# Attention and recurrence in one TensorE order: dense products over all heads of a trip, a block's steps over four trips

## The chip, the cores and the metric

One core of a Trainium2 chip runs the kernel. The metric is the time of one execution on the device, in microseconds (us). TensorE (PE) multiplies, VectorE (DVE) and ScalarE (ACT) do elementwise work, GpSimd (POOL) and SyncE (SP) mostly issue DMAs. Each engine takes its own list of instructions in order and waits on semaphores.

## The reference, cut to what matters

```python
# x is [8, 512, 512]; 16 heads of 32; cond is [8, 512]
qkv = x @ c_attn_w + c_attn_b                      # split into q, k_word, v_word
k = concat([cond @ uk_w.T + uk_b, k_word]);  v = concat([cond @ uv_w.T + uv_b, v_word])
scores = einsum('bhqd,bhkd->bhqk', q, k) / sqrt(32)    # causal, the image key is always seen
out = softmax(scores + mask) @ v
x = x + (out @ c_proj_w + c_proj_b)
xw = x @ Wx + b                                     # then 512 steps in sequence, h0 = cond:
h[t] = tanh(h[t-1] @ Wh + xw[:, t])
return x + h
```

Everything is float32; the products with c_attn_w and c_proj_w are made of three products of split operands (high x high, high x low, low x high).

## The kernel before

The 512 positions are four blocks of 128. A *trip* is one block of one pair of batches: 16 trips, trip g has block g // 4 and pair g % 4. A trip has 32 *heads* (two batches x 16 heads), so there are 512 heads in all, u = 32 g + h.

Work of a trip: `xsplit` splits x into high and low parts (ACT, then VectorE); `q` and `k` are projected in four chunks c of four heads each, `imgscore` scores chunk c against the image key; `v` are four products (two batches e, two halves). q and k go through DRAM (`kq_dram`) and come back as tiles of four heads of one batch: `kqload` of group 8 g + 4 e + c, two tile buffers. Values are stored by GpSimd (`vstore`) and come back by `vload`, three buffers, eight groups a trip. Per head: `score` (L839), shift against mask and image score (VectorE, L687), exp (ACT, L551), `turn` (transposes of the probabilities, L847, four heads later), a copy (L696 or L558), and per four heads `pv` (L860, ten heads later). Per batch: `total` (VectorE, L705 to L713, needs the trip before's x1 stores, as L713 overwrites their buffer), `imgturn`, `rowturn`, `norm`. When a trip's heads are done, `finish` does it inside the next trip: `proj` (four products), `x1n` (two transposes, copied by ACT, stored by GpSimd at L500), `wx` (four products into xw) or, in the last block, `keep` (a GpSimd copy, L490).

The recurrence has 512 `step`s. A step is 16 small products on TensorE (L924), a transpose (L751) and an add (L761) on VectorE, a tanh on ACT (L593); the next needs its result. Steps of block b need the x1 and xw of its four trips, so blocks 0 to 2's steps (128 each) run beside the attention of the next block; block 3's run alone at the end (the tail), with their own wx products (L916). After each 16 steps `out` turns and stores the states. wx of trip 4(b+1)+r overwrites the xw cells that steps 32 r to 32 r + 31 of block b read.

The order is planned by hand. `main_order` (L61) lists the events of all heads with a weight each (estimated us on TensorE). There, before the change, `project(g)` (L65) is the whole projection of a trip, `side` the list of dense events still to be placed: project(g + 1) is set at h = 0 and held until h = 10, when finish(g - 1) is put ahead of it; from there to h = 31 the list is spread over the heads. So heads 0 to 9 of a trip carry no dense event, heads 10 to 31 carry up to two each. `flush` (L82) adds the loads that are ready. `order` (L140) places each group of 32 steps, evenly by weight, between `finished` of trip group + 3 and the first wx of trip group + 4 (L149 to L158), and then gives every engine its own list, sorted by the planned clock plus a lag per engine and kind (`LAGS`, L45). SyncE's list has the loads and the q/k stores (L427, L439, L449), GpSimd's the mask loads (L476 to L482, two per trip, one for each batch of the next trip, after heads 15 and 31), vstore (L497), x1 stores (L500), keep and the output (L467, L505). Both wait in order, so what stands behind a waiting entry waits too.

Of the kernel before, what the change touches and what calls it, by code (L numbers as in the profile page):

```python
# [5 lines left out]
P = 128  # L6
# [44 lines left out]
    "SP": {"xload": 0.8, "vimgload": 0.5, "q": 1.3, "k": 1.3, "kqload": 0.0, "vload": 0.5},  # L51
# [5 lines left out]
def block_of(g):  # L57
    return g // PAIRS


def main_order():  # L61

    out = []

    def project(g):  # L65
        return ([("xsplit", g, k, 0.0) for k in range(2)]
                + [e for c in (0, 1) for e in (("q", g, c, 1.4), ("k", g, c, 1.4), ("imgscore", g, c, 0.5))]
                + [("v", g, i, 1.4) for i in range(4)] + [("vstore", g, 0, 0.0)]
                + [e for c in (2, 3) for e in (("q", g, c, 1.4), ("k", g, c, 1.4), ("imgscore", g, c, 0.5))])

    def finish(g):
        last = "keep" if block_of(g) == BLOCKS - 1 else "wx"
        return ([("proj", g, c, 1.4) for c in range(C)] + [("xload", g + 2, 0, 0.0)] * (g + 2 < TRIPS)
                + [("x1n", g, e, 0.85) for e in range(2)]
                + [(last, g, c, 1.7 * (last == "wx")) for c in range(C)] + [("finished", g, 0, 0.0)])

    out += [("xload", 0, 0, 0.0), ("xload", 1, 0, 0.0), ("mskload", 0, 0, 0.0), ("mskload", 0, 1, 0.0),
            ("vimgload", 0, 0, 0.0), ("vimgload", 0, 1, 0.0)] + project(0)
    side, loads = [], [("kqload", group, 0, 0.0) for group in range(TILES)]
    loads += [("vload", group, 0, 0.0) for group in range(VTILES)]  # L80

    def flush():  # L82

        ready = {(kind, g, i) for kind, g, i, _ in out[-200:]}
        for load in list(loads):
            trip, c = load[1] // 8, load[1] % C
            after = ("k", trip, c) if load[0] == "kqload" else ("vstore", trip, 0)
            if after in ready or load[1] % 8 > C:
                out.append(load)
                loads.remove(load)  # L90

    for u in range(HEADS + 2 * H):
        g, h = divmod(u, UNITS)
        if h == 0 and g < TRIPS:
            out += side
            flush()
            side = project(g + 1) if g + 1 < TRIPS else []
        if h == 10 and g:
            side = finish(g - 1) + side
# [886 lines left out]
```

## Time and profile before

| | us |
|---|---|
| median of 3 runs | 1851.33 (1847.14 to 1851.88) |
| the profiled execution | 1850.24, span 1848.5 |
| TensorE busy | 1657.4 (90%) |
| VectorE / ScalarE / GpSimd busy | 889.7 / 708.1 / 149.4 |
| mean granted TensorE clock | 0.948 |

"Busy" is the time with at least one instruction of the engine running; matmuls overlap, so 90% is not 90% of the peak. The clock is a share of 2.4 GHz: 1.00 is the full level, 0.50 the lower one of 1.2 GHz. The first attention head starts at 76 us, the last trip's heads end at 1527 us, and the tail of 128 steps starts at 1568 us.

### The profile page before, as it was taken

The page shows a single profiled execution, that of the slowest core. Times are in us where ns is not written, and L with a number is a line of the kernel's source. Part 1 is how long each engine was busy: PE and PEld are TensorE (multiplying, and loading weights), DVE is VectorE, ACT ScalarE, POOL GpSimd, SP SyncE. Part 2 cuts the span into 40 slices and gives each one's busy share as a digit, 9 for nine tenths or more (in the row PEclk, how much of TensorE's full clock was granted, in tenths as well). Part 3 has the DMA queues.
Part 4 walks back from the last instruction along what each step waited for, and adds up shares of the span by engine and source line. Part 5 has one row for each costly group of instructions (what it writes and reads, how often), then busy time and mean ns, then how long its engine had stood idle before and what let it go on. Part 6 is the DMA issues. An engine that isn't in the chain of part 4 may idle for free.

```text
span 1848.5 us, 67862 instructions
## 1 busy us (share of the span) xinstructions
PE 1657.4 (90%) x29292; PEld 1389.1 (75%) x29292; DVE 889.7 (48%) x2986; ACT 708.1 (38%) x2205; POOL 149.4 (8%) x248
## 2 busy tenths in 40 slices
PE   3788888989898998989899998989999887999997
PEld 2777777878787887878787886878778666888875
DVE  4254345454555454655645555556656563222222
ACT  2254444444443444444444444444444442111110
POOL 1001000000000000001011000001000000000000
PEclk7879888999999999999999998999999999999998
DMA  6455346444445355565555456566656640100000
GB/s 233 143 149 157 114 139 170 127 131 120 122 118 135 103 134 129 139 141 137 150 138 148 116 136 151 140 161 157 159 145 161 137 111 25 27 15 17 26 15 20
DMA packets 228442, 221.67 MB, mean 120 GB/s; under 512 B 22952, under 2 KB 187048, under 8 KB 227632
## 3 DMA queue, kind: packets, MB, share of 16 engines
q1 hardware_dynamic: 211568, 175.86, 36.7%
q0 software_dynamic: 16576, 41.46, 8.0%
q8 instruction: 233, 3.82, 0.9%
q14 instruction: 65, 0.53, 0.1%
HBM read 141.45 MB, written 75.76 MB: 118 GB/s over the span
## 4 chain that ended last, share of the span: by engine, by line
PE 72%; DMA 9%; DVE 8%; issue 5%; ACT 4%; SPq 3%; POOL 0%; DVEq 0%; POOLq 0%; ACTq 0%
PE rec L924 22%; PE turned L847 8%; PE dense L380 7%; DMA kq<-kq_dram 6%; PE dense L381 6%; PE dense L382 6%; PE dense L895 5%; PE scores L839 4%; PE pv L860 4%; PE scores L924 3%; DVE pre L751 3%; PE pv L878 2%; ACT hist L593 2%; DVE probs L687 1%; SPq L427 1%
## 5 line engine op out<-in xcount | busy, mean ns | idle before, releaser
L924 PE MATMUL rec<-wh,hist 128*8 128x128 f32 x14336 | 487.9, 277 | 29.7 <-ACT hist L593 23.3
L924 PEld LDWEIGHTS rec<-wh,hist 128*8 128x8 f32 x14336 | 356.2, 94 | 112.6 <-ACT hist L593 66.1
L551 ACT ACTIVATE probs<-probs,nmax 128x128 f32<-128x128 f32 (+3 forms) x512 | 287.2, 561 | 187.2 <-DVE nmax L687 179.6
L593 ACT ACTIVATE hist<-pre 128x32 f32<-128x32 f32 x512 | 131.7, 257 | 573.4 <-DVE pre L761 331.9
L687 DVE CUSTOM_DVE_ANT_0 probs<-scores,msk,nimg 128x128 f32<-128x128 f32 (+3 forms) x512 | 276.2, 545 | 131.2 <-PE scores L839 128.6
L839 PE MATMUL scores<-kq 96*128 96x128 f32 (+3 forms) x512 | 212.5, 420 | 82.6 <-DMA kq<-kq_dram 81.0
L751 DVE STREAM_TRANSPOSE pre<-rec 128x128 f32<-128x128 f32 x448 | 141.4, 316 | 295.6 <-PE rec L924 292.2
L847 PE MATMUL turned<-ident,probs 128*128 128x128 f32 x1280 | 250.0, 296 | 1.4 <-DVE probsT L696 1.0
L847 PEld LDWEIGHTS turned<-ident,probs 128*128 128x128 f32 x1280 | 150.3, 145 | 69.2 <-issue 56.7
L839 PEld LDWEIGHTS scores<-kq 96*128 96x128 f32 x512 | 107.7, 211 | 109.5 <-DMA kq<-kq_dram 86.8
L696 DVE COPY probsT<-turned 128x128 f32<-128x128 f32 (+3 forms) x256 | 124.8, 487 | 112.2 <-PE turned L847 111.6
L380 PE MATMUL dense<-xT_hi,wqkv_hi 128*128 128x256 f32 x512 | 152.0, 297 | 28.8 <-DVE xT_lo L653 23.9
L558 ACT COPY probsT<-turned 128x128 f32<-128x128 f32 (+3 forms) x256 | 107.6, 420 | 128.9 <-PE turned L847 128.0
L381 PE MATMUL dense<-xT_lo,wqkv_hi 128*128 128x256 f32 x512 | 146.0, 285 | 0.0
L382 PE MATMUL dense<-xT_hi,wqkv_lo 128*128 128x256 f32 x512 | 145.5, 284 | 0.0
L380 PEld LDWEIGHTS dense<-xT_hi,wqkv_hi 128*128 128x128 f32 x512 | 98.5, 192 | 38.2 <-issue 30.6
L860 PE MATMUL pv<-probsT,vbuf 128*32 128x128 f32 x2560 | 102.4, 290 | 0.3
L381 PEld LDWEIGHTS dense<-xT_lo,wqkv_hi 128*128 128x128 f32 x512 | 98.6, 193 | 0.6
L382 PEld LDWEIGHTS dense<-xT_hi,wqkv_lo 128*128 128x128 f32 x512 | 98.4, 192 | 0.0
L551 ACT ACTIVATION_READ_ACCUMULATOR probs<-probs,nmax 128x1 f32 x512 | 96.0, 188 | 0.0
L895 PE MATMUL dense<-x1T,wx 128*128 128x256 f32 x384 | 90.3, 383 | 0.7 <-ACT x1nat L586 0.3
L761 DVE TENSOR_TENSOR pre<-pre,xw 128x32 f32<-128x32 f32 x384 | 83.1, 216 | 13.1
(119 smaller groups left out, 2291.1 us busy)
## 6 DMA issues: line engine op xcount, KB each, us to landing
kq<-kq_dram SPq DMA_DIRECT2D x96, 320.0 KB, 5.7
kq<-kq_dram SPq DMA_DIRECT2D x96, 256.0 KB, 4.8
kq<-kq_dram SPq DMA_DIRECT2D x96, 192.0 KB, 3.7
kq_dram<-qs_hi SPq DMA_DIRECT2D x128, 128.0 KB, 2.1
kq_dram<-ks_hi SPq DMA_DIRECT2D x128, 128.0 KB, 3.2
kq<-kq_dram SPq DMA_DIRECT2D x96, 128.0 KB, 2.6
xin<-x SPq DMA_DIRECT2D x32, 256.0 KB, 3.1
kq_dram<-qs_lo SPq DMA_DIRECT2D x64, 128.0 KB, 2.4
```

Source lines behind the costliest of these rows:

```text
L380: pe.matmul(out, hi, moving_hi, start=first, stop=False)
L381: pe.matmul(out, hi, moving_lo, start=False, stop=False)
L382: return pe.matmul(out, lo, moving_hi, start=False, stop=last)
L551: act.activation(probs[:, g % PROBS, 0:n], probs[:, g % PROBS, 0:n], ACT.Exp, scale=-1.0, bias=nmax[:, e, h:h + 1], accum_out=rowsum[:, e, ...
L593: act.activation(hist[:, g // HALF % 2, :, :, g % HALF], pre[:, :, 0:B], ACT.Tanh).then_inc(h_ready, 1)
L687: dve.tensor_tensor_reduce(out=probs[:, g % PROBS, 0:n], in0=scores[g % 2][:, 0:n], in1=msk[:, e, 0:n], scale=-SCALE, scalar=nimg[:, trip ...
L751: dve.transpose(pre_all, rec_bank(g)[:, 0:P]).then_inc(rec_turned, 1)
L839: pe.matmul(scores[g % 2][:, 0:n], heads_tile(group)[0:3 * Q, j, 0:P], heads_tile(group)[0:3 * Q, j, P:P + n], start=True, stop=True).then ...
L847: last = pe.transpose(turned[g % 2][:, P * k:P * k + P], probs[:, g % PROBS, P * k:P * k + P], ident[:])
L860: last = pe.matmul(pv[Q * j:Q * j + Q, P * c:P * c + P], vtile[g % VTILES][:, k, Q * j:Q * j + Q], probsT[:, (HC * g + j) % TURNED, P * k: ...
L895: last = pe.matmul(d[:, 0:2 * P], wx[:, f, P * i:P * i + P], x1T[:, f, :], start=f == 0, stop=f == C - 1)
L924: last = pe.matmul(d[Q * j:Q * j + B, 0:P], hist[:, before // HALF, f, :, before % HALF], wh[:, f, P * j:P * j + P], start=f == 0 and not ...
```

## The change

Dense events are placed in two parts. Heads 0 to 9 of trip g now take values(g, 0), chunk(g, 3), values(g, 1): the trip's own four value products and its last chunk of q and k. Heads 10 to 31 take finish(g - 1), the split of the next x (ahead of the last two wx) and chunks 0 to 2 of trip g + 1, one event per head. Before the first head only chunks 0 to 2 of trip 0 are projected. Each value half is stored by itself, with a semaphore of its own. Loads are listed as soon as what they read is listed. A block's 128 steps are spaced evenly by weight over one window, from `finished` of trip 4 b + 3 to the first wx (or keep) of trip 4 b + 7; where a group's cells are about to be overwritten, its remaining steps are placed just before. Weights and three of SyncE's lags are changed, and the shift waits for its own chunk's image scores.

```diff
--- before.py
+++ after.py
@@ -48,7 +48,7 @@
     "ACT": {"xsplit": 0.0, "q": 0.2, "k": 0.2, "score": 0.8, "turn": 0.2, "imgprob": 0.2, "imgturn": 0.2,
             "rowturn": 0.2, "norm": 0.6, "wx": 0.2, "x1n": 0.2, "step": 0.7},
     "POOL": {"mskload": 0.0, "keep": 0.2, "vstore": 1.0, "x1n": 0.8, "finished": 0.0, "out": 1.0},
-    "SP": {"xload": 0.8, "vimgload": 0.5, "q": 1.3, "k": 1.3, "kqload": 0.0, "vload": 0.5},
+    "SP": {"xload": 0.8, "vimgload": 0.9, "q": 1.3, "k": 1.3, "kqload": 1.4, "vload": 0.5},
 }
 
 DENSE_KINDS = ("q", "k", "v", "imgscore", "imgturn", "rowturn", "proj", "wx", "x1n", "out")
@@ -60,80 +60,79 @@
 
 def main_order():
 
-    out = []
-
-    def project(g):
-        return ([("xsplit", g, k, 0.0) for k in range(2)]
-                + [e for c in (0, 1) for e in (("q", g, c, 1.4), ("k", g, c, 1.4), ("imgscore", g, c, 0.5))]
-                + [("v", g, i, 1.4) for i in range(4)] + [("vstore", g, 0, 0.0)]
-                + [e for c in (2, 3) for e in (("q", g, c, 1.4), ("k", g, c, 1.4), ("imgscore", g, c, 0.5))])
+    out, seen, loads = [], set(), [("kqload", group, 0, 0.0) for group in range(TILES)]
+    loads += [("vload", group, 0, 0.0) for group in range(VTILES)]
+
+    def emit(events):
+
+        for event in events:
+            out.append(event)
+            seen.add(event[:3])
+            for load in list(loads):
+                trip, k = divmod(load[1], 8)
+                if (("k", trip, k % C) if load[0] == "kqload" else ("vstore", trip, k // C)) in seen:
+                    out.append(load)
+                    loads.remove(load)
+
+    def chunk(g, c):
+        return [("q", g, c, 1.5), ("k", g, c, 1.5), ("imgscore", g, c, 0.5)]
+
+    def values(g, e):
+        return [("v", g, 2 * e, 1.5), ("v", g, 2 * e + 1, 1.5), ("vstore", g, e, 0.0)]
+
+    def begin(g):
+        return [("xsplit", g, k, 0.0) for k in range(2)]
 
     def finish(g):
         last = "keep" if block_of(g) == BLOCKS - 1 else "wx"
-        return ([("proj", g, c, 1.4) for c in range(C)] + [("xload", g + 2, 0, 0.0)] * (g + 2 < TRIPS)
-                + [("x1n", g, e, 0.85) for e in range(2)]
-                + [(last, g, c, 1.7 * (last == "wx")) for c in range(C)] + [("finished", g, 0, 0.0)])
-
-    out += [("xload", 0, 0, 0.0), ("xload", 1, 0, 0.0), ("mskload", 0, 0, 0.0), ("mskload", 0, 1, 0.0),
-            ("vimgload", 0, 0, 0.0), ("vimgload", 0, 1, 0.0)] + project(0)
-    side, loads = [], [("kqload", group, 0, 0.0) for group in range(TILES)]
-    loads += [("vload", group, 0, 0.0) for group in range(VTILES)]
-
-    def flush():
-
-        ready = {(kind, g, i) for kind, g, i, _ in out[-200:]}
-        for load in list(loads):
-            trip, c = load[1] // 8, load[1] % C
-            after = ("k", trip, c) if load[0] == "kqload" else ("vstore", trip, 0)
-            if after in ready or load[1] % 8 > C:
-                out.append(load)
-                loads.remove(load)
-
+        return ([("proj", g, c, 1.5) for c in range(C)] + [("xload", g + 2, 0, 0.0)] * (g + 2 < TRIPS)
+                + [("x1n", g, e, 0.55) for e in range(2)]
+                + [(last, g, c, 1.8 * (last == "wx")) for c in range(C)] + [("finished", g, 0, 0.0)])
+
+    emit([("xload", 0, 0, 0.0), ("xload", 1, 0, 0.0), ("mskload", 0, 0, 0.0), ("mskload", 0, 1, 0.0),
+          ("vimgload", 0, 0, 0.0), ("vimgload", 0, 1, 0.0)] + begin(0) + chunk(0, 0) + chunk(0, 1) + chunk(0, 2))
+    side, until = [], 0
     for u in range(HEADS + 2 * H):
         g, h = divmod(u, UNITS)
+        block, h2 = divmod(u, H)
         if h == 0 and g < TRIPS:
-            out += side
-            flush()
-            side = project(g + 1) if g + 1 < TRIPS else []
-        if h == 10 and g:
-            side = finish(g - 1) + side
-        block, h2 = divmod(u, H)
+
+            side, until = values(g, 0) + chunk(g, 3) + values(g, 1), 9
+        if h == 10:
+            side, until = [], UNITS - 1
+            if 0 < g <= TRIPS:
+                side += finish(g - 1)
+            if g + 1 < TRIPS:
+
+                at = max(len(side) - 3, 0)
+                side[at:at] = begin(g + 1)
+                side += chunk(g + 1, 0) + chunk(g + 1, 1) + chunk(g + 1, 2)
         if h2 == 8 and 0 < block <= 2 * TRIPS:
-            out.append(("norm", block - 1, 0, 0.9))
+            emit([("norm", block - 1, 0, 0.9)])
             if block + 1 < 2 * TRIPS:
-                out.append(("vimgload", (block + 1) // 2, (block + 1) % 2, 0.0))
+                emit([("vimgload", (block + 1) // 2, (block + 1) % 2, 0.0)])
         if h2 == 9 and 0 < block <= 2 * TRIPS:
-            out.append(("attnlow", block - 1, 0, 0.0))
-        p = block_of(min(g, TRIPS - 1))
+            emit([("attnlow", block - 1, 0, 0.0)])
         if u >= PV_LAG and (u - PV_LAG) % HC == 0 and u - PV_LAG < HEADS:
-            v = u - PV_LAG
-            out.append(("pv", v // HC, 0, 0.05 + 0.213 * (block_of(v // UNITS) + 1)))
-            if v // HC + VTILES < GROUPS:
-                loads.append(("vload", v // HC + VTILES, 0, 0.0))
+            v = (u - PV_LAG) // HC
+            if v + VTILES < GROUPS:
+                loads.append(("vload", v + VTILES, 0, 0.0))
+            emit([("pv", v, 0, 0.1 + 0.213 * (block_of(v // 8) + 1))])
         if TURN_LAG <= u < HEADS + TURN_LAG:
             v = u - TURN_LAG
-            out.append(("turn", v, 0, 0.11 * (block_of(v // UNITS) + 1)))
+            emit([("turn", v, 0, 0.05 + 0.11 * (block_of(v // UNITS) + 1))])
         if u < HEADS:
-            out.append(("score", u, 0, max(0.11, 0.053 * (p + 1)) + 0.06))
             if u % HC == HC - 1 and u // HC + TILES < GROUPS:
                 loads.append(("kqload", u // HC + TILES, 0, 0.0))
+            emit([("score", u, 0, max(0.11, 0.053 * (block_of(g) + 1)) + 0.1)])
             if h2 == 15 and block + 2 < 2 * TRIPS:
-                out.append(("mskload", (block + 2) // 2, block % 2, 0.0))
+                emit([("mskload", (block + 2) // 2, block % 2, 0.0)])
         if 0 < block <= 2 * TRIPS:
-            out += {1: [("imgprob", block - 1, 0, 0.0)], 2: [("total", block - 1, 0, 0.0)],
-                    4: [("imgturn", block - 1, 0, 0.15)], 5: [("rowturn", block - 1, 0, 0.45)]}.get(h2, [])
-        if g < TRIPS:
-            room = UNITS - 1 - h
-            take = len(side) if room == 0 else -(-len(side) // (room + 1))
-            if h < 10 and g:
-
-                take = 0
-            out += side[:take]
-            side = side[take:]
-        else:
-            out += side
-            side = []
-        flush()
+            emit({1: [("imgprob", block - 1, 0, 0.0)], 2: [("total", block - 1, 0, 0.0)],
+                  4: [("imgturn", block - 1, 0, 0.15)], 5: [("rowturn", block - 1, 0, 0.5)]}.get(h2, []))
+        take = len(side) if g >= TRIPS or h >= until else -(-len(side) // (until + 1 - h))
+        emit(side[:take])
+        side = side[take:]
     return out
 
 
@@ -146,16 +145,18 @@
         if kind in ("wx", "keep"):
             begins.setdefault(g, n)
     place = {}
-    for group in range((BLOCKS - 1) * PAIRS):
-        first, last = ends[group + PAIRS - 1] + 1, begins[group + PAIRS]
+    for b in range(BLOCKS - 1):
+
+        first, last = ends[(b + 1) * PAIRS - 1] + 1, begins[(b + 2) * PAIRS - 1]
         whole = sum(w for *_, w in main[first:last])
         done, n = 0.0, 0
         for at in range(first, last):
             done += main[at][3]
-            while n < STEPS and done >= whole * (n + 0.5) / STEPS:
-                place.setdefault(at, []).append(group * STEPS + n)
+            while n < P and (done >= whole * (n + 0.5) / P
+                             or at + 1 == begins.get((b + 1) * PAIRS + n // STEPS)):
+                place.setdefault(at, []).append(b * P + n)
                 n += 1
-        assert n == STEPS
+        assert n == P
 
     plan = {name: [] for name in ("PE", "DVE", "ACT", "POOL", "SP")}
     clock = 0.0
@@ -169,7 +170,7 @@
                 plan[name].append((clock + lags[kind], kind, g, i))
 
     def step(t):
-        put("step", t, 0, 0.85)
+        put("step", t, 0, 1.05)
         if t % HALF == 1 and t > HALF:
             put("out", t // HALF - 1, 0, 0.5)
 
...
                     trip, k = divmod(g, 8)
                     p, r = divmod(trip, PAIRS)
                     e, c = divmod(k, C)
-                    sp.wait_ge(v_stored, 32 * (trip + 1))
+                    sp.wait_ge(v_stored[e], 16 * (trip + 1))
                     if g >= VTILES:
                         sp.wait_ge(pv_done, g - VTILES + 1)
...
                 elif kind == "vstore":
-                    for n in range(4):
-                        wait_copied(pool, "v", g, n)
-                    for e in range(2):
-                        pool.dma_start(v_dram[2 * r + e, P * p:P * p + P, :], vnew[:, e, :]).then_inc(v_stored, 16)
+                    for n in range(2):
+                        wait_copied(pool, "v", g, 2 * i + n)
+                    pool.dma_start(v_dram[2 * r + i, P * p:P * p + P, :], vnew[:, i, :]).then_inc(v_stored[i], 16)
...
                 elif kind == "v":
                     wait_dense(dve, kind, g, i)
-                    if i == 0:
+                    e, half = divmod(i, 2)
+                    if half == 0:
                         dve.wait_ge(bv_loaded, 16)
                         if g:
-                            dve.wait_ge(v_stored, 32 * g)
-                    e, half = divmod(i, 2)
+                            dve.wait_ge(v_stored[e], 16 * g)
                     cols = slice(half * D // 2, (half + 1) * D // 2)
                     dve.tensor_tensor(vnew[:, e, cols], bank(kind, g, i)[:, 0:D // 2], bv[:, cols], ALU.add
                                       ).then_inc(copied(kind, g, i), 1)
...
                     if h == 0:
                         dve.wait_ge(mask_ready, 2 * trip + e + 1)
-                        wait_copied(dve, "imgscore", trip, C - 2)
-                        wait_copied(dve, "imgscore", trip, C - 1)
+                    if h % HC == 0:
+                        wait_copied(dve, "imgscore", trip, h // HC)
                     dve.tensor_tensor_reduce(out=probs[:, g % PROBS, 0:n], in0=scores[g % 2][:, 0:n],
                                              in1=msk[:, e, 0:n], scale=-SCALE, scalar=nimg[:, trip % 2, e, h:h + 1],
```

## Rows read from the trace of the kernel before

**Rows 1.** The page: busy us by engine, and TensorE's clock in 40 slices.
```profile
PE 1657.4 (90%) x29292; PEld 1389.1 (75%) x29292; DVE 889.7 (48%) x2986; ACT 708.1 (38%) x2205; POOL 149.4 (8%) x248
...
PEclk7879888999999999999999998999999999999998
```

**Rows 2.** TensorE's waits: us in total, times, longest.
```profile
PE scores L839 <- DMA kq<-kq_dram: 81.0, 20, 6.3
PE dense L380 <- DVE xT_lo L653: 23.9, 11, 15.5
PE rec L924 <- ACT hist L593: 23.3, 45, 1.4
```

**Rows 3.** Busy us per stretch, trips 9, 15: PE PEld DVE ACT POOL, clock, DMA, GB/s.
```profile
795.50:900.60 105.10, 99.14 (x1629) 82.68 (x1627) 57.78 (x185) 46.72 (x138) 9.21 (x14) 0.97 0.54 136
...
1436.60:1527.40 90.80, 77.36 (x1429) 60.08 (x1427) 55.20 (x157) 43.69 (x121) 7.11 (x12) 0.94 0.54 124
```

**Rows 4.** TensorE in time (start us, us, line) [idle before], trip 8, heads 0 to 4.
```profile
691.27 0.42 PE L839 MATMUL scores<-kq 96*128 96x384 f32 x1
...
694.06 0.42 PE L839 MATMUL scores<-kq 96*128 96x384 f32 x1
...
695.10 1.06 PE L924 MATMUL rec<-wh,hist 128*8 128x128 f32 x32
701.99 0.69 PE L839 MATMUL scores<-kq 96*128 96x384 f32 x1 [5.82 <-DMA kq<-kq_dram]
```

**Rows 5.** The same stretch: GpSimd's mask load and SyncE's tile loads.
```profile
691.78 0.58 POOL L476 DMA_DIRECT2D msk<-mask  x1
...
692.16 4.08 SPq L439 DMA_DIRECT2D kq<-kq_dram  x6
```

**Rows 6.** Busy us per stretch: the gap of trip 8, and behind it.
```profile
696.20:702.00 5.80, 0.01 (x1) 0.02 (x1) 1.11 (x5) 0.71 (x2) 1.62 (x2) 0.72 1.04 221
702.00:705.60 3.60, 3.60 (x30) 2.92 (x34) 1.25 (x4) 2.36 (x7) 0.00 (x0) 0.50 0.78 154
```

**Rows 7.** TensorE in time, trip 2: a product at the lower and full clock.
```profile
195.95 0.41 PE L382 MATMUL dense<-attnT_hi,wproj_lo 128*128 128x256 f32 x1
196.16 0.41 PE L380 MATMUL dense<-attnT_hi,wproj_hi 128*128 128x256 f32 x1
...
201.26 0.28 PE L381 MATMUL dense<-attnT_lo,wproj_hi 128*128 128x256 f32 x1
201.38 0.28 PE L382 MATMUL dense<-attnT_hi,wproj_lo 128*128 128x256 f32 x1
```

**Rows 8.** Busy us per stretch: one of block 0's four at the lower clock.
```profile
310.00:324.00 14.00, 10.18 (x62) 8.32 (x63) 6.10 (x22) 6.03 (x21) 1.30 (x2) 0.52 0.72 178
```

**Rows 9.** TensorE in time, the drain: two steps with nothing between them.
```profile
1544.18 1.07 PE L924 MATMUL rec<-wh,hist 128*8 128x128 f32 x32
1546.22 1.07 PE L924 MATMUL rec<-wh,hist 128*8 128x128 f32 x32 [0.97 <-ACT hist L593]
```

**Rows 10.** Busy us per stretch: the end of the drain.
```profile
1546.00:1568.00 22.00, 15.40 (x332) 12.30 (x332) 6.65 (x22) 3.37 (x12) 2.56 (x6) 1.00 0.07 26
```

**Rows 11.** Trip 13 in time: head 15's score, GpSimd's mask load, VectorE's L713.
```profile
1269.91 0.47 PE L839 MATMUL scores<-kq 96*128 96x512 f32 x1
...
1271.84 0.54 POOL L476 DMA_DIRECT2D msk<-mask  x1 [1.59 <-DVE nmax L687]
...
1281.39 0.46 POOL L482 TENSOR_TENSOR msk<-msk,causal 128x128 f32<-128x128 f32 x1
...
1282.99 0.43 DVE L713 COPY x1nat<-rinv 128x512 f32<-128x512 f32 x1
```

**Rows 12.** Trip 15 in time, VectorE's wait for the x1 store.
```profile
1490.00 0.43 DVE L713 COPY x1nat<-rinv 128x512 f32<-128x512 f32 x1 [1.72 <-DMA x_dram<-x1nat]
```

**Rows 13.** The page's DMA issues: count, KB each, median us to landing.
```profile
kq<-kq_dram SPq DMA_DIRECT2D x96, 320.0 KB, 5.7
...
x_dram<-x1nat POOLq DMA_DIRECT2D x32, 256.0 KB, 2.6
```

More of the change, by code:

```diff
@@ L315, in attention_recurrence @@
         tile_loaded = [sem(f"tile_loaded{i}") for i in range(TILES)]
-        v_stored = sem("v_stored")
+        v_stored = [sem(f"v_stored{e}") for e in range(2)]
         v_loaded = [sem(f"v_loaded{i}") for i in range(VTILES)]
@@ L508, in _ @@
             pool.wait_ge(out_stored, 16 * OUTS)
-            pool.wait_ge(v_stored, 32 * TRIPS)
+            for e in range(2):
+                pool.wait_ge(v_stored[e], 16 * TRIPS)
             pool.wait_ge(x1_stored, 32 * TRIPS)
@@ L743, in _ @@
                         dve.wait_ge(x1_kept, C * PAIRS)
-                        dve.wait_ge(v_stored, 32 * TRIPS)
+                        for e in range(2):
+                            dve.wait_ge(v_stored[e], 16 * TRIPS)
                     elif g % P == 0:
```

## Prediction, made blind

> **What bounds the kernel now.** I read the busy shares first, then what TensorE waited for, then one trip of the attention in order of time. TensorE is busy 90% of the span and its clock row shows dips all along [rows 1]; no other engine is above 48%. Inside the trips the share is higher still: trip 9 takes 105.10 us with 99.14 busy, at a mean clock of 0.97 [rows 3]. So nearly all that can be won without removing matmuls is TensorE's idle time, and the change removes none: the same products, transposes and steps are issued. The list of its waits says where the idle time is: 81.0 us in 20 waits for a load of the q/k tile, 23.9 us for the low part of x (15.5 of it once, in the set-up), 23.3 us in 45 waits of a recurrence step for the state before it [rows 2].
>
> The tile wait has one place, shown by trip 8 [rows 4]: the first four heads run from 691.27 to 694.06, a step follows at 695.10, and then TensorE is idle 5.82 us, till 701.99. Every later trip has the same gap once. The cause is the order of work: heads 0 to 9 of a trip carry no dense product, so its first four heads pass in some 4 us, while the next tile's load, issued at 692.16 [rows 5] just behind the last chunk's stores and beside a mask broadcast, lands only at 701.99. The DMA engines are full in the gap (share 1.04), and the clock then stays at its lower level for the 3.60 us behind it [rows 6].
>
> **What the order becomes.** Counted from the code: heads 0 to 9 of each trip carry its own four value products and chunk 3 (six products of 1.5 and one image score); from head 10 follow proj, x1n, wx and the next trip's chunks 0 to 2, one event per head. Steps are spaced evenly over four trips.
>
> **1. Tile wait: -73.** Heads 0 to 3 now hold two value products, attention work and three to four steps. A product is 12 matmuls at 0.12 us, 1.43 us, and a step is 1.0 us of TensorE [rows 7, 9], so the four heads take some 5.5 us in block 0 and 9 to 14 later, against some 4 now. A tile load lands in 5.7 us at its largest (320 KB) when it meets no jam [rows 13], and the second tile's load of that trip start, which shared the engines with it, is now issued those many us later. What stays: SyncE's queue now has the value loads, which wait for values stored in this very trip, ahead of the load of group 2; in block 0, where heads are short, I work it out as about 2 us late in each of trips 0 to 3. 81.0 - 8 = 73. Bounds: 2 us left in all (-79), 40 left (-41).
>
> **2. Clock: -13.** At the lower level a dense product's matmuls start 0.21 us apart, at the full one 0.12 [rows 7], so a product costs 1.1 us more. Block 0 has four long stretches at the lower level (the last one in [rows 8]); some nine products lie in the parts behind the waits: 10 us. The short stretch of each later trip [rows 6] holds transposes and steps, which cost nearly the same at either level: 12 x 0.25 = 3. Bounds -5 and -25.
>
> **3. Waits for the low part of x: -7.** The split of x moves ahead of the last two wx products, so two heads and 3.6 us lie before the first q. 23.9 - 15.5 = 8.4 [rows 2], of which I keep 1. Bounds -4, -8.
>
> **4. Waits of steps outside bursts: -11.** By the planner's weights, steps in block 1 now come every 1.71 instead of 1.39, and the last 32 steps of block 2 are not squeezed into trip 15 and the drain (13.4 us of idle time in trip 15, [rows 3]). Of 23.3 us I take half. Bounds 0 and -20.
>
> **5. Bursts of steps: +21.** This speaks against the change. An even spacing over the window of four trips is slower than the old one over each trip, but the 32 steps of a group must be done before wx of the matching trip overwrites their cells, and the placement forces the remainder there. Adding the weights (block 1: 57.0 a trip, window 218.8, 1.709 per step; 45.2 before the first wx) gives 26 steps placed and 6 forced, back to back, in head 16 of trip 5; 4 in trip 6, 3 in trip 7; the same 6, 4, 3 in trips 9 to 11; none in the last block, whose keep copies weigh nothing. Back to back, a step starts 2.04 us after the one before (1544.18 to 1546.22) and needs 1.0 of it [rows 9]: transpose, add and tanh lie between. TensorE issues in order, so everything behind waits: (5+3+2) x 2 = 20 extra x 1.04 = 21. Bounds 15 (something slips between) and 30 (VectorE busy with a shift when the step ends).
>
> **6. GpSimd's queue in mid-trip: +12.** x1n moves from heads 12 and 13 to 14 and 15. The mask load of head 15 has lag 0, x1n's store lag 0.8, so on GpSimd the load now stands ahead of the store, and its issue, wait and two operations hold the queue. In trip 13 head 15's score starts at 1269.91 and GpSimd is through with the mask at 1281.85 [rows 11]; a store behind that lands 2.6 us later [rows 13], at +14.6 us. VectorE's copy L713 at head 18 waits for exactly this store, with scores, transposed copies and steps queued behind it. It stands at 1282.99, +13.1 [rows 11]; without the two products and the output transpose that lie there now, at about +9.5. So VectorE is 5 us late. The trace has one such wait, 1.72 us in trip 15 [rows 12]. By the same working: trips 1 to 3 some 1.1 us, trips 4, 8 and 12 about 2, trips 13 and 14 about 5; behind a burst none. Sum 19.7; TensorE's work in hand covers about 1 us of each of the eight: 12. Bounds 0 and 30.
>
> Sum: -73 -13 -7 -11 +21 +12 = -71. The profiled execution took 1850.24 us (span 1848.5); 1850.2 - 71 = 1779.2. The median is 1.1 above it: **1780 us**. SyncE's other moves (kqload's lag 1.4, the image values') come off at nothing: its queue waits on engines now and will again. VectorE's wait for chunk 3's image scores (made in head 5, used in head 12), the two semaphores of stored values (same order on GpSimd) and the one-event-per-head spreading of products, for which two PSUM banks suffice today, are costed at nothing as well: VectorE is busy 55% and ACT 44% of trip 9 [rows 3]; if that cover were gone, each product would cost TensorE up to 1 us of waiting for its bank. The setup gains nothing beyond the first tile wait: six products leave the part before the first head and come back inside trip 0.
>
> A rule that speaks against the bursts: the Trainium skill, "TensorE: Matmul & The Clock Gate", section "A second HAM failure mode: psum-queue depth-cycling", says that frequent micro-idles between groups of matmuls can make the clock swing between its levels. By it a burst would be followed by dense work at 1.2 GHz. The trace does not bear it out: in the drain, with steps waiting on each other and 15.40 of 22 us busy, the clock is 1.00 [rows 10].
>
> **Rivals.**
> A. GpSimd's queue costs nothing and the clock comes back whole: 1780 - 12 - 8 = 1760. For it: TensorE's lead may cover short waits. Against: the 5 us of trips 13 and 14 are too long for that. 0.2.
> B. Half of the tile wait stays, because the value loads block SyncE at trip starts and the jam of mask, stores and loads is as it was. Tile term -41 and clock -5: 1780 + 32 + 8 = 1820. For it: full DMA engines in the gap [rows 6]. Against: twice the time until the tile is due. 0.17.
> C. Each burst drops the clock. Six stretches of the length of rows 6 (6.8 us from the gap's middle), full of dense work at 0.21 instead of 0.12, lose 3 us each: 1780 + 18 = 1798. Against: [rows 10]. 0.08.
> D. Slower: the tile wait moves from group 1 to group 2 of each trip at its full size. Group 2's load stands on SyncE behind value loads that wait for the store of this trip's values; that store stands on GpSimd behind the mask load of head 31. It decides once stored values land later than score 8 less 7 us (load and issue); worse than before from 4.6 us a trip on. Then terms 1 and 2 are zero: 1850 - 7 - 11 + 21 + 12 = 1865, 1866 by the median. Against: between head 31 and score 8 lie 20 us of TensorE work in block 1 and 30 in block 3, mask plus store take 10 to 14. 0.05.
>
> **How the numbers follow.** Forecast 0.5, A 0.2, B 0.17, C 0.08, D 0.05. The range leaves D out and part of A's and B's outer bounds: 1750 to 1824. A measurement can tell 0.3%, 5.5 us, from no change. Faster 0.93 (all but D, less a little for B's tail), same 0.02, slower 0.05.
>
> **What would show it.** Right: TensorE's wait for q/k tiles under 20 us; windows of trips 1 to 15 without the gap after head 3; clock 1.00 through trips 4 to 11; six places with 6, 4, 3 steps 2.04 us apart, in head 16; VectorE's L713 waiting for the x1 store, about 5 us in trips 13 and 14. Wrong: tile waits at another group, long waits of SyncE for stored values with TensorE idle behind them, or a mean clock no higher than before.

## The result: 1800.4 us, and the profile after

The changed kernel takes 1800.41 us (median of 4 runs, 1796.14 to 1802.70) against 1849.24 for the kernel before in the same comparison: a ratio of 0.973, 95% interval 0.971 to 0.976. The forecast was 1780 in a range of 1750 to 1824. The sign and the largest term were right, and the gain was 49 us where 71 were expected. The profiled execution has a span of 1798.5, so against [rows 1]'s span of 1848.5 there are 50.0 us to explain.

The page after: busy us by engine, and TensorE's clock in 40 slices.

```profile
span 1798.5 us, 67877 instructions
...
PE 1634.6 (91%) x29292; PEld 1378.1 (77%) x29292; DVE 888.8 (49%) x2986; ACT 709.9 (39%) x2205; POOL 149.6 (8%) x248
...
PEclk8988989999999999999999999998998999999999
```

Against [rows 1] the matmuls are the same 29292, yet they keep TensorE busy 22.8 us less (1657.4 to 1634.6). That is the clock: by its records TensorE was busy 132 us at the lower level before and is 92 now, and with a step's 1.07 us at the full level for 1.90 at the lower one (rows below) that is some 18 of the 22.8, an estimate. The other 27.2 us are idle time (191.1 to 163.9). The clock row has few dips left, and some of them are new: an 8 in slices 28 and 31, where the row before has nines.

TensorE's waits after, to be read against [rows 2] (us in total, times, longest).

```profile
PE rec L926 <- ACT hist L594: 56.6, 70, 7.8
...
PE scores L841 <- DVE nmax L688: 23.7, 6, 5.6
...
PE scores L841 <- DMA kq<-kq_dram: 13.8, 11, 4.4
...
PE dense L381 <- DVE xT_lo L654: 4.6, 1, 4.6
```

The tile wait fell from 81.0 to 13.8, and the wait for the low part of x from 23.9 to 4.6. What came up is the first two rows: steps waiting for a state (23.3 before, with 1.4 as the longest; 56.6 now, with 7.8) and scores waiting for a shift on VectorE (1.5 in the same view of before, 23.7 now). The changes of these four rows sum to -67.2 - 19.3 + 33.3 + 22.2 = -31.0, near the 27.2 of idle time.

The start of trip 8 after, which answers [rows 4]: TensorE in order of time (start us, us).

```profile
650.89 0.42 PE L841 MATMUL scores<-kq 96*128 96x384 f32 x1
...
652.67 1.07 PE L926 MATMUL rec<-wh,hist 128*8 128x128 f32 x32
...
653.86 0.42 PE L841 MATMUL scores<-kq 96*128 96x384 f32 x1
...
658.67 0.44 PE L841 MATMUL scores<-kq 96*128 96x384 f32 x1
...
659.09 0.42 PE L841 MATMUL scores<-kq 96*128 96x384 f32 x1
...
662.60 0.42 PE L841 MATMUL scores<-kq 96*128 96x384 f32 x1
```

Head 4 now starts 11.7 us after head 0 (9 to 14 were worked out) and waits for nothing. It had been 10.7 us before, 5.8 of them idle. The products that fill this time no longer stand in the rest of the trip.

What took their place is seen in trip 13. GpSimd and VectorE in order of time, and last the step that TensorE resumes with; in brackets the idle time before each and who ended it.

```profile
1235.05 0.54 POOL L477 DMA_DIRECT2D msk<-mask  x1 [1.55 <-DVE nmax L688]
...
1241.66 0.25 DVE L708 RECIPROCAL rinv<-total 128x16 f32<-128x16 f32 x1
...
1242.57 0.45 POOL L483 TENSOR_TENSOR msk<-msk,causal 128x128 f32<-128x128 f32 x1
...
1242.96 0.60 POOL L500 DMA_DIRECT2D x_dram<-x1nat  x1
...
1248.66 0.43 DVE L714 COPY x1nat<-rinv 128x512 f32<-128x512 f32 x1 [6.74 <-DMA x_dram<-x1nat]
...
1250.50 1.90 PE L926 MATMUL rec<-wh,hist 128*8 128x128 f32 x32 [6.10 <-ACT hist L594]
```

And the same stretch by windows (busy us of PE, PEld, DVE, ACT, POOL; then clock, DMA share, GB/s).

```profile
1241.00:1249.00 8.00, 2.31 (x27) 1.43 (x15) 1.23 (x5) 1.35 (x4) 3.47 (x5) 0.74 0.85 222
1249.00:1255.00 6.00, 4.50 (x60) 3.15 (x64) 4.92 (x14) 3.34 (x10) 2.16 (x4) 0.50 0.16 45
1255.00:1262.30 7.30, 7.30 (x141) 6.16 (x134) 4.00 (x12) 3.54 (x11) 0.00 (x0) 0.99 0.57 141
```

GpSimd issues the mask load at 1235.05, waits for it, does its two operations, and only then issues the second of the trip's two x1 stores, at 1242.96. VectorE's copy L714 overwrites what the store reads, so it starts 5.7 us later, at 1248.66, and the shifts, transposes and adds queued behind it hold TensorE for 6.10 us. Behind the gap the clock is at its lower level (0.50) for 6 us. VectorE's row for this wait, over the whole kernel, is this one:

```profile
  DMA x_dram<-x1nat: 44.9, 8
```

There are eight such waits, in trips 1 to 4, 8 and 12 to 14, and before there was only the one of 1.72 us [rows 12].

### The profile page after: what moved, and what is told of

It is laid out like the page before. It is cut to its first block, busy times and chain, and to the rows that moved or that the text cites. A ratio compares the mean times of both kernels' runs of the same rounds, so it can differ in the third digit from the quotient of the medians.

```text
span 1798.5 us, 67877 instructions
## 1 busy us (share of the span) xinstructions
PE 1634.6 (91%) x29292; PEld 1378.1 (77%) x29292; DVE 888.8 (49%) x2986; ACT 709.9 (39%) x2205; POOL 149.6 (8%) x248
## 4 chain that ended last, share of the span: by engine, by line
PE 72%; DVE 9%; DMA 7%; issue 5%; ACT 4%; SPq 2%; POOL 1%; DVEq 0%; POOLq 0%; ACTq 0%
PE rec L926 24%; PE turned L849 8%; PE dense L381 7%; PE dense L382 6%; PE dense L383 6%; PE pv L862 4%; PE scores L841 4%; PE scores L926 3%; PE dense L897 3%; DVE pre L753 3%; ACT hist L594 3%; DMA msk<-mask 2%; DMA x_dram<-x1nat 2%; PE pv L880 2%; DVE probs L688 1%
## 5 line engine op out<-in xcount | busy, mean ns | idle before, releaser
L926 PE MATMUL rec<-wh,hist 128*8 128x128 f32 x14336 | 483.7, 275 | 62.9 <-ACT hist L594 56.6
L849 PE MATMUL turned<-ident,probs 128*128 128x128 f32 x1280 | 241.0, 288 | 1.9 <-DVE probsT L697 0.9
L841 PE MATMUL scores<-kq 96*128 96x128 f32 (+3 forms) x512 | 203.8, 403 | 37.7 <-DVE nmax L688 23.7
L849 PEld LDWEIGHTS turned<-ident,probs 128*128 128x128 f32 x1280 | 145.3, 141 | 65.3 <-issue 55.2
L841 PEld LDWEIGHTS scores<-kq 96*128 96x128 f32 x512 | 102.4, 201 | 58.2 <-DVE nmax L688 27.8
L897 PE MATMUL dense<-x1T,wx 128*128 128x256 f32 x384 | 104.3, 419 | 6.4 <-ACT xw L582 6.4
L862 PE MATMUL pv<-probsT,vbuf 128*32 128x128 f32 x2560 | 98.6, 282 | 1.4 <-DVE x1T L728 1.3
L897 PEld LDWEIGHTS dense<-x1T,wx 128*128 128x128 f32 x384 | 76.9, 209 | 21.7 <-ACT xw L582 9.3
```

The source lines that it names most:

```text
L841: pe.matmul(scores[g % 2][:, 0:n], heads_tile(group)[0:3 * Q, j, 0:P], heads_tile(group)[0:3 * Q, j, P:P + n], start=True, stop=True).then ...
L849: last = pe.transpose(turned[g % 2][:, P * k:P * k + P], probs[:, g % PROBS, P * k:P * k + P], ident[:])
L862: last = pe.matmul(pv[Q * j:Q * j + Q, P * c:P * c + P], vtile[g % VTILES][:, k, Q * j:Q * j + Q], probsT[:, (HC * g + j) % TURNED, P * k: ...
L897: last = pe.matmul(d[:, 0:2 * P], wx[:, f, P * i:P * i + P], x1T[:, f, :], start=f == 0, stop=f == C - 1)
L926: last = pe.matmul(d[Q * j:Q * j + B, 0:P], hist[:, before // HALF, f, :, before % HALF], wh[:, f, P * j:P * j + P], start=f == 0 and not ...
```

## Experiments

Edits are against the changed kernel, except where "before" is said. Ratios are to the kernel before, with 95% intervals.

### The x1 store ahead of the mask load (changed kernel)

```diff
-    "POOL": {"mskload": 0.0, "keep": 0.2, ...
+    "POOL": {"mskload": 2.5, "keep": 0.2, ...
```

> The changed kernel with GpSimd's mask loads 2.5 later in its list, so that both x1 stores stand ahead of the mask load of head 15. Theory: VectorE's wait for the x1 store (44.9 us, 8 times) goes to under 3, and most of it is TensorE time: 23.7 us of waits for VectorE's shifts and some 10 of the step waits, so 1800 - 30 = 1770. Rival (the size in the prediction, 12 us): TensorE's work in hand hides most of it: 1788. A second rival: the masks, now later, are late for the heads: no gain.

Measured: 1744.80, ratio 0.944 [0.941, 0.947], span 1743.1, that is 55 us below the changed kernel, nearly twice what was expected. Its page has this row of busy times:

```profile
PE 1615.2 (93%) x29292; PEld 1366.6 (78%) x29292; DVE 890.1 (51%) x2986; ACT 709.3 (41%) x2205; POOL 151.7 (9%) x248
```

And these are TensorE's first two waits:

```profile
PE rec L926 <- ACT hist L594: 45.0, 72, 1.2
PE scores L841 <- DMA kq<-kq_dram: 13.3, 10, 4.5
```

The longest wait of a step is 1.2 (1.4 before), the scores' wait for a shift is gone from the list, and VectorE's wait at L714 is 0.6 us once. The gain lies where it should: heads 16 to 23 of the eight trips take 21.1, 20.6, 20.2, 24.6, 28.2, 30.7, 26.9 and 29.0 us in the changed kernel, and 14.5, 16.9, 13.9, 17.7, 20.9, 23.6, 18.7 and 19.9 here, a sum of 55 us. Idle time falls by 36.0 (163.9 to 127.9) and busy time by 19.4. In the eight stretches alone idle time falls by 35 and busy time by 20. So a third of the store wait's price was the clock behind each gap.

### No bursts (changed kernel)

Each group's 32 steps are spread up to their own deadline, so none is forced.

```diff
-        first, last = ends[(b + 1) * PAIRS - 1] + 1, begins[(b + 2) * PAIRS - 1]
-        whole = sum(w for *_, w in main[first:last])
...
+        at, n = ends[(b + 1) * PAIRS - 1] + 1, 0
+        for r in range(PAIRS):
+            last = begins[(b + 1) * PAIRS + r]
+            whole, done = sum(w for *_, w in main[at:last]), 0.0
```

> The changed kernel with each group of 32 steps spaced evenly up to its own deadline (the first wx that overwrites its cells), so none is forced: in block 1 the first group gets one step per 1.41 of weight, the others one per 1.78. Theory: the 20 extra steps of the bursts cost 1.04 us each, so the step waits fall from 56.6 to about 35 and the time by 21: 1779. Rival: what the bursts lose is won back in the step-free stretch behind them: no change, 1800.

Measured: 1794.66, ratio 0.970 [0.965, 0.973]: 6 us below the changed kernel where 21 were expected. TensorE's first two waits tell why.

```profile
PE scores L842 <- DVE nmax L689: 40.5, 10, 8.7
PE rec L927 <- ACT hist L595: 30.4, 53, 2.8
```

The steps' waits halved, but the scores' wait for VectorE rose from 23.7 to 40.5. Most of that rise is a change of name: in trips 13 and 14 a step waited 6.1 and 7.8 us for the late store, and now a score waits 8.4 and 8.7 for it. VectorE's own row shows how much more of the late store came up:

```profile
DVE x1nat L715 <- DMA x_dram<-x1nat: 49.2, 10, 7.9
```

Against 44.9 in 8 waits, that is two more, of 1.2 and 2.8 us, in trips 10 and 11: the burst of head 16 had stood ahead of L714 there and had covered the same store. From the first score of trip 4 to that of trip 12 the run is 8.8 us shorter. But it also changed something else: the last block's steps are bound to their trips again, 6 more of them are left behind the last score, and the tail takes 12.3 us more (316.5 against 304.2). So this run doesn't price the bursts, and the next ones have the store first.

### Both together

The two edits above in one kernel.

> Both edits, stores ahead of the mask load and no bursts. Theory: the two costs are apart in place (bursts in trips 5 to 7 and 9 to 11; store waits in the other trips), so the gains add: 1800 - 30 - 21 = 1749. Rival: bursts covered the store wait in their trips, so without them it comes up there, and with the stores first that does not matter; then the second edit alone (e4) gains less than 21 and both together still about 50.

Measured: 1731.99, ratio 0.937 [0.934, 0.941], span 1727.2, 17 us below the expectation. Against the run with the store first alone it is 13 us by the medians. So the bursts cost more than the 6 of the run above showed, though here too the tail is 12.5 us longer (313.7 against 301.2).

### Store first, and bursts taken out of blocks 1 and 2 only

As above, but the last of the three blocks keeps the changed kernel's even spacing over four trips, so its last steps aren't squeezed.

```diff
+        at, n, size = ends[(b + 1) * PAIRS - 1] + 1, 0, P if b == BLOCKS - 2 else STEPS
+        for r in range(P // size):
```

> The changed kernel with the stores ahead of the mask load and no bursts, but the steps of block 2 spaced evenly over their whole window as in the changed kernel (there no deadline forces any), so that they are not squeezed into the drain. Theory: trips 0 to 11 as with both edits, from trip 12 on as with the stores first alone: 1008.1 + (1743.1 - 1035.0) = 1716 span, 1720. Rival: the last block's two variants differ for another reason than the spacing: 1732.

Measured: 1729.46, ratio 0.936 [0.934, 0.939], the lowest median here, though too close to the run with both edits (0.937) to be told from it. It is 71 us below the changed kernel and 9 above the expectation. From its page:

```profile
span 1726.1 us, 67877 instructions
...
PE 1612.1 (93%) x29292; PEld 1362.2 (79%) x29292; DVE 889.1 (52%) x2986; ACT 708.6 (41%) x2205; POOL 151.1 (9%) x248
```

And TensorE's waits for states and tiles:

```profile
PE rec L927 <- ACT hist L595: 29.3, 53, 1.5
PE scores L842 <- DMA kq<-kq_dram: 13.8, 10, 4.4
```

This and the run with the store first differ by the bursts alone. From the first score of trip 4 to that of trip 12 they take 750.9 and 773.3 us: the bursts cost 22.4 us. In the six trips with bursts the difference is 29.0; trips 4 and 8, which have the denser steps when no burst takes the rest, give 6.5 back. Of the 22.4, 17.4 are idle time and 5.0 busy time. The whole spans differ by 17.0 only, since the tail behind the last score took 307.1 us here and 301.2 there. Of these 5.9, 3.9 lie behind the issue of the last output store (10.7 us to the end here, 6.8 there), and in the other 2.0 stands one stretch of 3.4 us at the lower clock that the other run doesn't have. Why either differs isn't shown.

### The old placement of steps, store first (changed kernel)

```diff
-    for b in range(BLOCKS - 1):
...
+    for group in range((BLOCKS - 1) * PAIRS):
+        first, last = ends[group + PAIRS - 1] + 1, begins[group + PAIRS]
```

> The changed kernel with the stores ahead of the mask load and the old placement of the steps (each group of 32 between the end of one finish and the first wx of the next), to be set beside the stores first alone (1744.8). Theory: no bursts (-13, as both edits showed), but steps every 1.43 of weight, none in heads 16 to 22, and the last group squeezed into the end of trip 15 and the drain, where each step costs 2.04 us and not 1.0 (+20): about 1752. Rival: the even spacing over the heads of wx is what fills TensorE: 1775 or more.

Measured: 1754.49, ratio 0.949 [0.947, 0.951], as expected. TensorE's waits:

```profile
PE rec L924 <- ACT hist L592: 39.8, 77, 1.8
PE scores L839 <- DMA kq<-kq_dram: 17.0, 13, 4.5
```

The new placement is worth 10 us even with its bursts (1744.80), and 25 without (1729.46). The row also shows something that no term of the forecast had: with the old placement the steps wait 39.8 us where the kernel before has 23.3 [rows 2]. In trips 4 to 14, heads 0 to 13 hold 13.9 us of these waits (3.0 before) and heads 24 to 31 hold 15.6 (5.8 before). In the first of these the removed gaps had perhaps given the chain of steps time to catch up; in the second no gap had stood. No run separates the causes.

### Only the new placement of steps (before)

```diff
-    for group in range((BLOCKS - 1) * PAIRS):
...
+    for b in range(BLOCKS - 1):
```

> The kernel before with only the steps' new placement (a block's 128 steps evenly over four trips). By the old weights 4, 2 and 1 steps are forced in blocks 1 and 2, 8 us of extra waits; trip 15 and the drain win some 10 us of step waits; the tile wait stays at 81. Theory: the placement alone is worth nothing, 1845 within 6. Rival: it is what brings the gain: 1820 or less.

Measured: 1845.86, ratio 0.999 [0.997, 1.001], as expected: alone, the placement does nothing that can be measured.

```profile
PE scores L841 <- DMA kq<-kq_dram: 65.7, 18, 6.8
PE dense L382 <- DVE xT_lo L655: 33.3, 14, 15.8
PE rec L926 <- ACT hist L595: 32.7, 55, 1.3
```

It takes 15 us from the tile waits and adds 9 to each of the other two.

### Only the image-value load behind the x loads (before)

```diff
-    "SP": {"xload": 0.8, "vimgload": 0.5, ...
+    "SP": {"xload": 0.8, "vimgload": 0.9, ...
```

> The kernel before with one number changed: SyncE's lag of the image values' load 0.5 -> 0.9, so that in the set-up the first two loads of x stand ahead of it. Theory: in the set-up SyncE sat at the image values' load, which waits for a store by GpSimd, with x behind it; the first dense product then starts at about 35 us instead of 46.3, and the time falls by 11 us (1838). Rival: the earlier start of the changed kernel comes from its shorter projection before the first head; then this edit gives nothing (within 2 us).

Measured: 1838.24, ratio 0.994 [0.993, 0.996]. The wait for the low part of x falls from 23.9 us with 15.5 as its longest [rows 2] to this:

```profile
PE dense L380 <- DVE xT_lo L653: 13.0, 11, 4.6
```

SyncE and ScalarE at the start of the kernel before:

```profile
34.99 0.85 SPq L418 DMA_DIRECT2D vimg<-vimg_dram  x2
35.88 2.25 SPq L411 DMA_DIRECT2D xin<-x  x4
...
44.69 1.14 ACT L531 CAST xT_hi<-xin 128x512 fp32r<-128x512 f32 x2 [16.93 <-DMA xin<-x]
```

And of this run:

```profile
20.61 1.86 SPq L411 DMA_DIRECT2D xin<-x  x4
37.04 0.81 SPq L418 DMA_DIRECT2D vimg<-vimg_dram  x2
...
26.88 1.13 ACT L531 CAST xT_hi<-xin 128x512 fp32r<-128x512 f32 x2
```

The image-value load waits for a store of GpSimd, and with lag 0.5 against the x loads' 0.8 it stood ahead of them on SyncE. A lag of 0.9 turns the two around, the x loads are issued 15 us earlier (and at 19.82 in the changed kernel), and the first head starts 10 us earlier, at 65.7 instead of 76.2.

### How much of the old gap is a jam on the DMA engines (before)

Three runs. In the first, the mask loads get a lag of 12.

```diff
-    "POOL": {"mskload": 0.0, ...
+    "POOL": {"mskload": 12.0, ...
```

> The kernel before with GpSimd's mask loads 12 later in its list: they no longer share the DMA engines with the tile load at a trip's start. It tells apart what the tile wait there was made of. Theory (short heads first of all, the jam on top): the load itself takes 4 to 6 us and the four heads 4, so some 50 of the 81.0 us of tile waits stay, and the time falls by 25 to 35 us. Rival, jam only: under 15 us stay, 1847 - 75. Rival, the mask does not matter: 81, 1847.

Measured: 1848.85, ratio 1.000 [0.999, 1.002]. This says nothing: the lag moved the load of head 15, but the one issued at the trip's start stayed beside the tile loads. So the mask load was held by a wait instead:

```diff
                         pool.wait_ge(shifted_ready, UNITS * (g - 1) + H * (i + 1))
+                        if i == 1:
+                            pool.wait_ge(scores_ready, UNITS * g + 6)
```

> The kernel before, with one thing changed: the mask broadcast for a trip's second batch, which is issued at each trip start beside the first tile loads, now waits until head 5 of the trip has been scored, so it lies behind the gap. It tells how much of the 81 us of tile waits is the jam on the DMA engines and how much is the order (too little work ahead of the tile). If the order makes the gap, which is my theory, the first load still takes its 5.7 us and is issued no earlier: tile waits stay at 55 us or more, and the time falls by 5 to 25 us. If the mask broadcast is what delays the tile, tile waits fall under 25 us, the clock at trip starts rises, and the time falls by 50 us or more.

Measured: 1836.42, ratio 0.994 [0.992, 0.996]. The tile waits, and then head 4 of trip 8 in time:

```profile
PE scores L841 <- DMA kq<-kq_dram: 72.9, 21, 6.4
```

```profile
690.72 0.69 PE L841 MATMUL scores<-kq 96*128 96x384 f32 x1 [4.80 <-DMA kq<-kq_dram]
```

Without the mask the gap of trip 8 is 4.80 instead of 5.82 us, and 8 of the 81 us go. In the third, the second tile load waits for the first to be used:

```diff
-                        sp.wait_ge(scores_ready, HC * (g - TILES + 1))
+                        sp.wait_ge(scores_ready, HC * (g - TILES + 1) + (g % 8 == 2))
```

> The kernel before, with one thing changed: the second tile load of each trip start (group 2) waits for one more score, so it is issued only when the tile that TensorE waits for has landed, and doesn't share the DMA engines with it. If the second load is what stretches the first one from 5.7 to nearly 10 us, the wait for group 1 falls by some 2 to 4 us a trip, but the same load is then late for group 2, so that the sum of tile waits stays between 70 and 100 us and the time within 1% of before. If the second load takes no part, group 1's wait stays at about 5.8 us a trip and group 2's is added: tile waits over 110 us and the time up by 30 us or more.

Measured: 1847.26, ratio 0.999 [0.998, 1.001], tile waits 78.9 us (81.0 before). Neither neighbour alone makes the gap. But the load was slow each time: from its first issue to its landing the awaited tile of trip 8 took 9.8 us before, 8.8 without the mask, 9.7 without the second tile, and 7.5 in the changed kernel. Its three parts have a median of 4.8 us on the page of before (96 loads of 256 KB). At that the last part, issued at 693.14, would have left some 1.8 of the 5.8 us of idle time, an estimate. What slows it isn't shown; a value load and GpSimd's reload of x1 are issued some 1 us ahead of it before and in both runs, and no run moves them. The order is what the change repaired, and it is enough: the old load landed 10.7 us after head 0, and head 4 now starts 11.7 after it.

## Why the prediction was right or wrong, step by step

| term | forecast | measured | from |
|---|---|---|---|
| 1 tile wait | -73 | -67 | waits before and after |
| 2 clock | -13 | -23; -45 in the fastest kernel | busy sums |
| set-up (not forecast) | 0 | -11 | longest x wait 15.5 to 4.6; -9 by the run with this load alone |
| 3 low part of x | -7 | -8 | waits, less the set-up's |
| 4 step waits outside bursts | -11 | +6; +1 and -2 by place | 23.3 before, 29.3 in the fastest kernel; 24.0 and 21.7 outside bursts and store gaps with the store first and in the changed kernel |
| 5 bursts | +21 | +22 (trips 4 to 11), +17 (span) | store first, with and without |
| 6 GpSimd's queue | +12 | +55 | store first |

From the kernel before to the fastest one the span falls by 122.4, and the first five rows give -67 - 45 - 11 - 8 + 6 = -125. The bursts then bring 17.0 back and the late store 55.4, which makes -50.0, the difference of the two spans. The rows overlap by a few us, so the rest isn't explained further.

That the forecast of -71 came within 21 us of this is luck in part. It had the store too low by 43 us and the steps' waits by 17; against that it missed 32 us of the clock and 11 of the set-up.

**1. Right.** The gap after head 3 is gone. The residual was to be 8 us, 2 in each of trips 0 to 3. It is 13.8: 9.5 in trip 0, with 4.4 as the longest, and the rest in five small waits later. One reason given for it failed: with the second tile's load out of the way the awaited one took 9.7 us, against 9.8.

**2. Wrong in the price of a lower clock.** The prediction costed the transposes and steps behind a gap as "nearly the same at either level". They aren't. The run with the store first shows a step at both levels; TensorE in order of time, trip 9:

```profile
769.84 1.07 PE L926 MATMUL rec<-wh,hist 128*8 128x128 f32 x32 [0.97 <-ACT hist L594]
771.88 1.07 PE L926 MATMUL rec<-wh,hist 128*8 128x128 f32 x32 [0.97 <-ACT hist L594]
773.92 1.64 PE L926 MATMUL rec<-wh,hist 128*8 128x128 f32 x32 [0.97 <-ACT hist L594]
776.50 1.90 PE L926 MATMUL rec<-wh,hist 128*8 128x128 f32 x32 [0.95 <-ACT hist L594]
779.38 1.90 PE L926 MATMUL rec<-wh,hist 128*8 128x128 f32 x32 [0.97 <-ACT hist L594]
781.21 3.61 PE L897 MATMUL dense<-x1T,wx 128*128 128x256 f32 x8
...
785.15 1.89 PE L897 MATMUL dense<-x1T,wx 128*128 128x256 f32 x8
```

A step takes 1.90 instead of 1.07. In trips 4 to 15 TensorE was busy 68 us at the lower level before and 3 in the fastest kernel. At 1.07 for 1.90 that is some 28 us (an estimate), where the forecast had 12 x 0.25 = 3. In all, the busy time of the same matmuls could fall by 45 us (1657.4 to 1612.1). The changed kernel got half of that, mostly because term 6 made new gaps with the lower level behind them.

**The set-up.** The step that failed is "SyncE's other moves (kqload's lag 1.4, the image values') come off at nothing: its queue waits on engines now and will again". I had asked what stands late on SyncE in a trip, not what stands first in its list. Two entries changed places there, and one of them waits for GpSimd.

**3. Right.** It was 8.4 us in ten small waits, and all ten are gone.

**4. Wrong: nothing was saved.** The new placement does save the expected amount, 39.8 to 29.3 us (-10.5). But I took 23.3 as the sum that it would be saved from. The old placement in the new, tighter order waits 39.8, 16.5 more, and why isn't shown. In the changed kernel 21.0 of the 56.6 us of step waits lie in the bursts and 13.9 in the store gaps of trips 13 and 14, which leaves 21.7 where 12 were expected.

**5. Right in place, count and size of the waits.** The steps' waits in the bursts are 21.0 us, as forecast. That the whole price, 22, is the same number is luck: the clock within some bursts, which the term left out, adds to it, and the thinner steps of trips 4 and 8 take from it. In the changed kernel as it stands, taking the bursts away gave only 8.8 in those trips. In head 16 of trips 5, 6, 7 and of 9, 10, 11 stand rows of 6, 5 and 4 steps 2.04 us apart: the forced 6, 4 and 3, the last two with one evenly placed step ahead. Rival C wasn't wholly wrong, since its mechanism exists: in the rows above the clock falls in the middle of a burst of six. It does not in every burst or execution (in the changed kernel it falls in trip 5's burst and not in trip 9's), so its price stays small: of the 22.4 us between the two runs 5.0 are busy time. [rows 10], on which I argued against it, shows steps that wait on each other at full clock, but in a stretch that holds other work as well. The Trainium skill, "TensorE: Matmul & The Clock Gate", section "A second HAM failure mode: psum-queue depth-cycling", says that frequent micro-idles can make the clock swing, and by these rows the trace agrees in some of the bursts.

**6. Right in place and count, wrong in size: 55 for 12.** The eight trips are the eight that were named, and none of the six behind bursts waits. Three figures of the working failed. (a) A store was to land 2.6 us after its issue, the page's median [rows 13]. The eight late ones took 3.1 to 5.6; the one of trip 13 ran at a DMA share of 0.85. That gives about 15 of the 25 us by which VectorE's eight waits, 44.9 in sum, exceed the 19.7 of the working; the other 10 lie mostly in trips 1 to 4, for which the forecast gives sums and no working, so what failed there stays open. (b) "TensorE's work in hand covers about 1 us of each" was a guess without a row. VectorE also transposes and adds for the steps and shifts the scores, so TensorE stops almost with it: 36 of the 45 us are TensorE idle time. (c) The clock behind each gap, 19 us, wasn't costed here, though I had read the same effect behind the tile gap [rows 6].

**Rivals.** B and D are refuted by the tile row of 13.8 us. D's mechanism is there without its price: SyncE does wait for stored values, and the tile loads behind it are in time all the same.

```profile
SPq L450 <- DMA v_dram<-vbuf: 120.6, 16, 16.0
```

A asked what the time would be if GpSimd's queue cost nothing: 1760. The run with the store first is that kernel, and it took 1745.

## What to carry to other kernels

When a store and a blocking load change places in an in-order queue, the store's reader can pay the load's whole wait, so list every queue in which two entries swap, the set-up's too; here two such swaps were worth 55 and 9 us. A gap is to be priced with the lower clock behind it, for every kind of matmul, and a landing time is to be read at the place where the DMA will run, not as a median. And an edit that is to price one cause must change that cause alone: the run without bursts showed 6 us of their 17 to 22, because it also made the tail longer, because a late store came up behind two of the bursts, and because the clock didn't fall in the same bursts in both executions.

## What the runs showed of the hardware

- A step (16 products in the code, 32 matmuls in the trace) takes 1.07 us at 2.4 GHz and 1.90 at 1.2 GHz (granted clock 0.50), start to start 2.04 and 2.88 with the same 0.97 of waiting.
- With TensorE busy 1.07 of every 2.04 us, the clock fell within some bursts of five or six steps, from the fourth or fifth step on, and not in others of the same program.
- The awaited q/k tile of trip 8 took 9.8 us to land before and 7.5 in the changed kernel; without the mask load beside it 8.8, without the second tile's load 9.7.
- The 256 KB x1 store has a median of 2.6 us to landing before and 3.1 after. In trip 13, where the DMA engines were 85% busy, the copy that waits for it started 5.7 us after its issue.
